# Self-attention's softmax maxima turned by 32x32 squares and two DRAM transfers instead of TensorE transposes, in a four-layer diffusion transformer

## The chip, the cores and the metric

The kernel runs on 1 core of one Trainium2 chip. The metric is the device time of one execution in microseconds, taken as the median of several; before the change it is 2573.73 us. All data is float32; some operands are float32r (a 4-byte format that TensorE multiplies faster), for which a value is split in a high and a low part so that nothing is lost.

## The reference

Sixteen batches of x [256 rows, 256 features] go through four layers. Layers 0, 2 and 3 are full: self-attention, cross-attention to a context of 120 rows, and an MLP. Layer 1 has cross-attention alone. Cut to a full layer and to layer 1:

```python
# layers 0, 2, 3 (16 heads of 16 features; N = 256 queries, S = 120 context rows)
mod = silu(cond) @ ada_w + ada_b                    # shifts, scales and gates, six rows
qkv = (ln(x) * (1 + scale_a) + shift_a) @ qkv_w + qkv_b
x = x + gate_a * (softmax(q @ k.T / 4) @ v @ proj_w + proj_b)
q = ln(x) @ q_w + q_b;  k, v = split(context @ kv_w + kv_b)
x = x + softmax(q @ k.T / 4) @ v @ cp_w + cp_b
x = x + gate_m * (gelu(mlp_in @ fc1_w + fc1_b) @ fc2_w + fc2_b)
# layer 1: adaptive layer norms of x and context, then the cross-attention line
```

The softmax subtracts each row's maximum. This kernel keeps that: it needs, for every query and head, the largest score over the keys.

## The kernel before, in words

**Jobs and steps.** The work on one batch in one layer is cut into steps, and each engine runs its part of the steps in one long order written out in tables of words (`START`, `TURN`, `WITH_L1`, `TAIL`). A word is a part and a step: P is the projection of self-attention's q, k and v, F its attention, A its output projection; R, G and B are the same for cross-attention; E is the MLP. A leading 1, as in 1G, means layer 1. One pass of a table is a turn; it works on different batches of all parts at once, so that TensorE has something to do while other engines finish a step. `TURN` is for turns without layer 1, `WITH_L1` for turns 3 to 21, in which layer 1's cross-attention (from turn 6 on) runs beside layer 0. There are 48 jobs of F and 64 of G, 16 of them of layer 1.

**Attention.** Steps S (L1287 on TensorE) multiply q with k, query rows on the partitions, into the four-bank PSUM tile `score`; VectorE reduces each to row maxima (`row_max`, L978). F has units S0 to S3, G has S0 and S1. `score` is one tile for all: the next unit on TensorE waits until the one before it is reduced. Steps T (L1309) multiply again, now with keys on the partitions, and L1314 subtracts the maxima inside PSUM, by a matmul of a selection matrix `sel` with `max_t`; ScalarE takes the exponential (`probs`, L1117). Steps PV (L1340) multiply with v, steps O (L1000 to L1011, VectorE) turn and normalise.

**The maxima.** Between S and T they must be turned: S leaves them with queries on the partitions, T needs them with heads on the partitions and queries along the row. Step X (VectorE, L987 and L990) negates them and splits them in a high and a low part, in `max_parts`, 8 columns of each group of 32. Step M transposes `max_parts` on TensorE (two 128x128 transposes by L1144, into one of three PSUM banks called the ring), and ScalarE copies the result to `max_t` (L1106). The first unit T0 waits for that copy.

**The ring.** The steps of most projections, norms and M take the three ring banks in turn; a step waits until the bank's last result was read.

**Queues.** All transfers are started by SyncE (SP) in order: the laying of q and k (L652, L661 to L663), loads of weights and context, and the gates `gate_now_P` and `gate_now_E` (L720, L721), 1 KB rows of DRAM spread to all partitions. `gate_now_P` waits for the product `gated` of A.PR (L1019 on VectorE), which reads its buffer. GpSimd (POOL) adds `gated` to x (L787, L793).

In the two tables the places that matter are

```python
TURN:     F.S3 E.H3 p.N P.gld A.PR F.X A.PR.d / G.S0 F.M B.PR B.PR.d R.C / G.S1 E.F20a E.F20b G.X / F.T0 ...
WITH_L1:  F.S2 P.gld E.H1 f.O1 E.H2 / F.S3 F.X 1R.LN E.RES E.H3 / 1G.S0 A.PR F.M A.PR.d /
          1G.S1 1G.X B.PR E.F20a / G.S0 E.F20b 1G.M B.PR.d / G.S1 E.F21a / 1G.T0 ... 1G.T1 ... F.T0
```

A word with `.d` is where SyncE, GpSimd and VectorE do their part of a step that TensorE and ScalarE did at the plain word. In the trace the places of M in `TURN` show TensorE in the order A.PR, G.S0, F.M, B.PR, R.C, G.S1.

Of the kernel before, what the change touches and what calls it, by code (L numbers as in the profile page):

```python
# [7 lines left out]
F32 = mybir.dt.float32  # L8
# [5 lines left out]
P = 128  # L14
# [4 lines left out]
NT = 256  # L19
# [14 lines left out]
CTX_LN = (False, True, False, True)  # L34

# [123 lines left out]

def turn(i, nb):  # L160
# [23 lines left out]
def sequence(nb):  # L184
# [11 lines left out]
    for r, m, step, n in steps:  # L196
        here = None
        if step in RING_STEPS:
# [61 lines left out]
def build_program(nc, a, out, nb=16):  # L260
# [9 lines left out]
    cross_order = {job: i for i, job in enumerate(cross_jobs)}  # L270
    normed_order = {job: i for i, job in enumerate(job for job in cross_jobs if CTX_LN[job[0]])}
# [8 lines left out]
    with ctx:  # L280
        def sb(name, shape, dt=F32):
# [7 lines left out]
        sel = sb("sel", [P, PAIRS])  # L289
        minus_half = sb("minus_half", [P, TT])  # L290
# [54 lines left out]
        max_parts = {r: sb(f"max_parts_{r}", [P, TT, P]) for r in "FG"}  # L345
        max_t = {r: sb(f"max_t_{r}", [P, NT]) for r in "FG"}
# [36 lines left out]
        m_psum = signals("m_psum", "FG")  # L383
# [11 lines left out]
        max_t_ready = signals("max_t_ready", "FG")  # L395
# [13 lines left out]
        max_parts_ready = signals("max_parts_ready", "FG")  # L409
        o_turned_ready = signals("o_turned_ready", "FG", 2)  # L410
# [18 lines left out]
        k_laid = semaphore("k_laid")  # L429
        x_stored = semaphore("x_stored")  # L430
# [154 lines left out]
        def _(sp):  # L585
# [211 lines left out]
        def _(dve):  # L797
# [6 lines left out]
                .then_inc(sel_ready, 1)  # L804

# [48 lines left out]
            for r, m, step, n, here in steps_d:  # L854
# [124 lines left out]
                elif step == "X":  # L979
                    src = row_max[r][:, :, :, :].rearrange("p t g c -> p (t g) c")  # L980
                    parts = max_parts[r][:, :, :].rearrange("p t (g w) -> p (t g) w", g=GROUPS)[:, :, 0:2 * PAIRS]\
# [3 lines left out]
                    m_psum[r].wait_before(dve, m, n)  # L985
# [6 lines left out]
                        .then_inc(max_parts_ready[r].sem, 1)  # L992
                elif step in ("O0", "O1"):
# [43 lines left out]
        def _(act):  # L1037
# [3 lines left out]
            for r, m, step, n, here in steps:  # L1041
# [61 lines left out]
                elif step == "M":  # L1103
# [36 lines left out]
        def _(pe):  # L1140
# [46 lines left out]
            for r, m, step, n, here in steps:  # L1187
# [103 lines left out]
                elif step == "M":  # L1291
# [4 lines left out]
                elif step[0] == "T" and step[1:].isdigit():  # L1296
# [4 lines left out]
                    if v == 0:  # L1301
                        pe.wait_ge(max_t_ready[r].sem, max_t_ready[r].after(m, n))
                        if m == 0 and n == 0:
                            pe.wait_ge(sel_ready, 1)
# [95 lines left out]
```

## Time and profile before

| what | value |
|---|---|
| median of 3 runs (lowest to highest) | 2573.73 us (2573.45 to 2574.57) |
| the profiled execution, its own time | 2577.71 us |
| its span in the trace | 2575.9 us |
| TensorE, busy | 2479.3 us, 96% |
| VectorE, ScalarE, GpSimd, busy | 72%, 49%, 18% |
| DMA queue of SyncE, share of 16 engines | 24.7% |

The busy shares say which engine could set the time. The view of waits says who waited for whom and how long in total. The timeline lists instructions in order of time with the idle time before them; a matmul's duration overlaps the next one's, so distances are read from start to start. The DMA view gives, for each transfer, the median time from its issue to its landing.

### The profile page before, as it was taken

The numbers are of one execution on the slowest core, as the hardware profiler recorded it, in microseconds if no ns is written. First come the engines' busy times: TensorE is split into PE (matmuls) and PEld (weight loads), VectorE is DVE, ScalarE is ACT, GpSimd is POOL, SyncE is SP. The second block draws the span as 40 slices with busy tenths as digits, with TensorE's granted clock in tenths as the row PEclk, the third lists the DMA queues.
The fourth block names the chain that finished last, engine by engine and source line by source line (L and its number), as shares of the span: only waits on it lengthen the run. The fifth ranks groups of instructions, "written<-read, shape, count | busy, mean of one in ns | idle before, by whom it ended". The sixth has DMA issues, their size and how long they took to land.

```text
span 2575.9 us, 66165 instructions
## 1 busy us (share of the span) xinstructions
PE 2479.3 (96%) x27466; PEld 1848.3 (72%) x27466; DVE 1858.5 (72%) x3532; ACT 1274.0 (49%) x1810; POOL 467.2 (18%) x510
## 2 busy tenths in 40 slices
PE   5779999999999999999999999999999999999998
PEld 3557777777777777777777777777777777777767
DVE  4767777777777777777777767777677677776752
ACT  1345544555555555555455554554555545445443
POOL 0111211212111211111121211211212212112121
PEclk7889999999999999999999999999999999999999
DMA  5322222222222223232122122132231222222211
GB/s 188 129 93 78 78 74 74 74 80 87 83 77 76 90 81 96 77 101 68 56 76 74 56 76 74 62 96 78 80 107 60 82 84 78 78 66 80 82 33 42
DMA packets 236749, 207.56 MB, mean 81 GB/s; under 512 B 87682, under 2 KB 222020, under 8 KB 236452
## 3 DMA queue, kind: packets, MB, share of 16 engines
q1 hardware_dynamic: 236452, 203.32, 24.7%
q8 instruction: 220, 3.60, 0.6%
q14 instruction: 77, 0.63, 0.1%
HBM read 58.34 MB, written 4.39 MB: 24 GB/s over the span
## 4 chain that ended last, share of the span: by engine, by line
PE 79%; DVE 12%; issue 3%; ACT 3%; SPq 2%; DMA 1%; POOL 1%; DVEq 0%; POOLq 0%; ACTq 0%
PE o_acc L1340 11%; PE score L1287 10%; PE ring L1371 10%; PE ring L1248 10%; PE ring L1362 10%; PE score L1309 8%; PE ring L1352 6%; DVE row_max_F L978 5%; DVE row_max_G L978 5%; PE ring L1144 4%; PE ring L1256 3%; PE score L1314 3%; PE ring L1268 2%; ACT probs L1117 2%; PE ring L1271 2%
## 5 line engine op out<-in xcount | busy, mean ns | idle before, releaser
L1117 ACT ACTIVATE probs<-score 120x2048 f32<-120x2048 f32 (+1 forms) x320 | 601.6, 1880 | 374.8 <-PE score L1314 368.0
L978 DVE TENSOR_REDUCE row_max_F<-score 128x8 f32<-128x2048 f32 x192 | 438.7, 2285 | 103.3 <-PE score L1287 102.8
L1371 PE MATMUL ring<-w_fc,h_t 128*128 128x256 f32 x1536 | 368.9, 386 | 1.0 <-ACT h_t L1128 1.0
L1362 PE MATMUL ring<-x_t_E,w_fc 128*128 128x256 f32 x1536 | 368.3, 386 | 0.0
L978 DVE TENSOR_REDUCE row_max_G<-score 128x16 f32<-128x1920 f32 x128 | 276.1, 2157 | 116.8 <-PE score L1287 116.8
L1128 ACT ACTIVATE h_t<-ring,cols 128x256 f32<-128x256 f32 x384 | 160.7, 470 | 341.1 <-PE ring L1362 341.0
L1362 PEld LDWEIGHTS ring<-x_t_E,w_fc 128*128 128x128 f32 x1536 | 280.8, 190 | 59.3 <-issue 20.3
L1000 DVE STREAM_TRANSPOSE o_turned<-o_acc 128x512 f32<-128x512 f32 x224 | 159.9, 714 | 220.3 <-PE o_acc L1340 220.3
L1371 PEld LDWEIGHTS ring<-w_fc,h_t 128*128 128x128 f32 x1536 | 282.5, 190 | 46.3 <-ACT h_t L1128 1.4
L1340 PE MATMUL o_acc<-probs,v_self 128*17 128x256 f32 x3072 | 204.3, 384 | 0.0
L793 POOL TENSOR_TENSOR x<-x,gated 128x256 f32<-128x256 f32 x96 | 70.3, 733 | 723.1 <-DVE gated L1032 723.1
L1248 PE MATMUL ring<-x_t_P,w_qk 128*128 128x256 f32 x768 | 197.8, 403 | 1.2 <-ACT x_t_P L1068 1.2
L1309 PE MATMUL score<-q_F,k_F 32*128 32x256 f32 x3072 | 166.6, 303 | 8.9 <-ACT probs L1117 5.7
L1309 PEld LDWEIGHTS score<-q_F,k_F 32*128 32x128 f32 x3072 | 119.3, 184 | 75.2 <-issue 55.7
L1248 PEld LDWEIGHTS ring<-x_t_P,w_qk 128*128 128x128 f32 x768 | 143.9, 197 | 35.2 <-issue 8.4
L1287 PEld LDWEIGHTS score<-k_F,q_F 32*128 32x128 f32 x3072 | 106.4, 188 | 84.2 <-DVE row_max_F L978 42.0
L1287 PE MATMUL score<-k_F,q_F 32*128 32x256 f32 x3072 | 146.3, 307 | 21.4 <-DVE row_max_F L978 18.5
L1287 PEld LDWEIGHTS score<-k_G,q_G 32*128 32x128 f32 x4096 | 125.3, 187 | 52.4 <-DVE row_max_G L978 28.0
L1287 PE MATMUL score<-k_G,q_G 32*128 32x120 f32 x4096 | 142.9, 277 | 14.8 <-DVE row_max_G L978 12.0
L787 POOL TENSOR_TENSOR x<-x,gated 128x512 f32<-128x512 f32 x48 | 60.8, 1267 | 423.0 <-DVE gated L1019 423.0
L1340 PE MATMUL o_acc<-probs,v_ctx 120*17 120x256 f32 x2048 | 135.5, 382 | 0.0
L1099 ACT ACTIVATE q_parts<-ring,cols 128x256 fp32r<-128x256 f32 x224 | 94.0, 472 | 80.9 <-PE ring L1248 78.9
(136 smaller groups left out, 3770.9 us busy)
## 6 DMA issues: line engine op xcount, KB each, us to landing
q_G<-q_parts SPq DMA_DIRECT2D x256, 128.0 KB, 2.1
q_F<-q_parts SPq DMA_DIRECT2D x192, 128.0 KB, 2.1
k_F<-k_parts SPq DMA_DIRECT2D x96, 256.0 KB, 2.5
k_F<-k_parts SPq DMA_DIRECT2D x192, 128.0 KB, 2.2
k_G<-k_parts SPq DMA_DIRECT2D x128, 120.0 KB, 2.2
k_G<-k_parts SPq DMA_DIRECT2D x256, 60.0 KB, 1.9
gate_now_P<-gate_rows SPq DMA_DIRECT2D x48, 256.0 KB, 3.2
gate_now_E<-gate_rows SPq DMA_DIRECT2D x48, 256.0 KB, 3.4
```

Of the source, the lines that this page charges most:

```text
L978: nc.vector.tensor_reduce(dst, src, AX.X, ALU.max).then_inc(row_max_ready[r].sem, 1)
L1000: nc.vector.transpose(o_turned[:, :, :, :].rearrange("p i b d -> p (i b d)"), o_acc[:, :])\
L1117: nc.scalar.activation(probs[v % 2][0:keys, :, :], score[0:keys, :].rearrange("p (h q) -> p h q", h=2 * GROUPS), ACT.Exp, scale=SCALE).the ...
L1128: last = nc.scalar.activation(h_t[:, c, :], ps[:, c % 2 * NT:(c % 2 + 1) * NT], ACT.Gelu_apprx_tanh, bias=col(m, "fc1", c))
L1144: return nc.tensor.transpose(dst, src, ident[0:rows_in, 0:rows_in])
L1248: last = mm(ps[:, c * NT:(c + 1) * NT], weight[:, k, at + c * P:at + (c + 1) * P], buffer(x_t, r, m, n)[:, k, :], start=k == 0, stop=k == ...
L1287: last = mm(score[:, col0:col0 + width], q_now[at, c, e, tile * P:(tile + 1) * P].bitcast(F32R), k_now[at, two, c, e, :].bitcast(F32R), st ...
L1309: mm(score[0:keys, g * BANK + e * NT:g * BANK + (e + 1) * NT], k_now[at, two, c, e, tile * P:tile * P + keys].bitcast(F32R), q_now[at, c, ...
L1340: last = mm(o_acc[32 * j:32 * j + HD + 1, i * NT:(i + 1) * NT], v_head, probs[v % 2][0:keys, 2 * j + i, :], start=tile == 0 and (i == 0 or ...
L1352: last = mm(ps[:, t * D:(t + 1) * D], buffer(o_t, r, m, n)[:, k, t * P:(t + 1) * P], weight[:, k, :], start=k == 0, stop=k == KC - 1)
L1362: last = mm(ps[:, c % 2 * NT:(c % 2 + 1) * NT], w_fc1[:, k, c * P:(c + 1) * P], buffer(x_t, r, m, n)[:, k, :], start=k == 0, stop=k == KC - 1)
L1371: last = mm(ps[:, 0:D], h_t[:, k, t * P:(t + 1) * P], w_fc2[:, k, :], start=k == 0, stop=k == MC - 1)
```

## The change

It concerns the maxima of self-attention from the fourth job on (45 of 48) and of layer 1's cross-attention (16 of 64). For these, X writes high and low parts packed in 32 columns, and VectorE transposes 128x64 in squares of 32x32. SyncE writes the squares to a DRAM tensor `max_rows` (32 heads' parts by 256 queries), at X, and at M reads it back into `max_t`, once for each of the four groups of partitions. TensorE's transposes and ScalarE's copy are gone there; the step M no longer takes a ring bank. T0 waits for the read. A second selection matrix, `sel_moved`, fits the new order of rows.

```diff
+def by_transfers(r, m, n, nb):
+    return (r == "F" and FULL_BEFORE[m] * nb + n >= 3) or (r == "G" and m == 1)
...
-        if step in RING_STEPS:
+        if step in RING_STEPS and not (step == "M" and by_transfers(r, m, n, nb)):
             here = at % RING
...
+        max_rows = {r: nc.dram_tensor(f"max_rows_{r}", [32, NT], F32, kind="Internal").ap() for r in "FG"}
...
+        max_turned = {r: sb(f"max_turned_{r}", [P, TT, 32]) for r in "FG"}
...
+                if step == "X" and by_transfers(r, m, n, nb):
+                    sp.wait_ge(max_turned_ready[r].sem, max_turned_ready[r].after(m, n))
+                    if moved_order[r][m, n] > 0:
+                        sp.wait_ge(max_laid[r].sem(m, n), max_laid[r].after(m, n) - 16)
+
+                    sp.dma_start(max_rows[r].rearrange("h (t a q) -> a h t q", t=TT, a=4), max_turned[r][:, :, :])\
+                        .then_inc(max_written[r].sem(m, n), 16)
+                elif step == "M" and by_transfers(r, m, n, nb):
+                    sp.wait_ge(max_written[r].sem(m, n), max_written[r].after(m, n))
+                    t_psum[r].wait_before(sp, m, n)
+                    sp.dma_start(max_t[r][:, :], max_rows[r].unsqueeze(0).to_broadcast([GROUPS, 32, NT]))\
+                        .then_inc(max_laid[r].sem(m, n), 16)
...
+            for g in range(GROUPS):
+                at = slice(32 * g, 32 * (g + 1))
+                last = nc.vector.tensor_reduce(pair_rows_moved[at, :], ident[at, 40 * g:40 * g + 2 * PAIRS]
+                                               .rearrange("p (c e) -> p c e", e=2), AX.X, ALU.add)
+            last.then_inc(pair_rows_ready, 1)
+            dve.wait_ge(pair_rows_ready, 2)
+            nc.vector.tensor_copy(sel_moved[:, :].bitcast(F32R), pair_rows_moved[:, :]).then_inc(sel_ready, 1)
...
+                    if by_transfers(r, m, n, nb):
+                        parts = max_parts[r][:, :, 0:32].rearrange("p t (b e) -> p t b e", e=2)
...
+                    if by_transfers(r, m, n, nb):
+                        dve.wait_ge(max_parts_ready[r].sem, max_parts_ready[r].after(m, n))
+                        if moved_order[r][m, n] > 0:
+                            dve.wait_ge(max_written[r].sem(m, n), max_written[r].after(m, n) - 16)
+                        nc.vector.transpose(max_turned[r][:, :, :],
+                                            max_parts[r][:, :, 0:32])\
+                            .then_inc(max_turned_ready[r].sem, 1)
...
-                elif step == "M":
+                elif step == "M" and not by_transfers(r, m, n, nb):
                     act.wait_ge(m_psum[r].sem, m_psum[r].after(m, n))
...
-                elif step == "M":
+                elif step == "M" and not by_transfers(r, m, n, nb):
                     pe.wait_ge(max_parts_ready[r].sem, max_parts_ready[r].after(m, n))
...
-                        pe.wait_ge(max_t_ready[r].sem, max_t_ready[r].after(m, n))
+                        if by_transfers(r, m, n, nb):
+                            pe.wait_ge(max_laid[r].sem(m, n), max_laid[r].after(m, n))
+                        else:
+                            pe.wait_ge(max_t_ready[r].sem, max_t_ready[r].after(m, n))
```

TensorE, the last turn with layer 1, from 1G.S0 to 1G.S1 (the brackets name the semaphores an instruction waits for), before:

```order
L1287 MATMUL score<-k_G,q_G 128x120 [waits k_laid,q_laid,row_max_ready_F]
L1287 MATMUL score<-k_G,q_G 128x120 x31
L1352 MATMUL ring<-w_proj,o_t_A 128x256 [waits o_t_ready_F,h_ready_E]
L1352 MATMUL ring<-w_proj,o_t_A 128x256 x3
L1144 MATMUL ring<-ident,max_parts_F 128x128 [waits max_parts_ready_F,h_ready_E]
L1144 MATMUL ring<-ident,max_parts_F 128x128
L1287 MATMUL score<-k_G,q_G 128x120 [waits row_max_ready_G]
```

and with the change:

```order
L1342 MATMUL score<-k_G,q_G 128x120 [waits k_laid,q_laid,row_max_ready_F]
L1342 MATMUL score<-k_G,q_G 128x120 x31
L1411 MATMUL ring<-w_proj,o_t_A 128x256 [waits o_t_ready_F,h_ready_E]
L1411 MATMUL ring<-w_proj,o_t_A 128x256 x3
L1342 MATMUL score<-k_G,q_G 128x120 [waits row_max_ready_G]
```

The two transposes are gone; what stands before and behind them waits for the same as before.

VectorE, a turn without layer 1, from the statistics of p.N to the reduction of G.S0, before and with the change:

```order
L825 TENSOR_SCALAR var_eps_P<-mean_var_P 128x2 [waits mean_ready_P]
L987 TENSOR_SCALAR max_parts_F<-row_max_F 128x8x4 [waits row_max_ready_F,m_psum_F]
L990 SCALAR_TENSOR_TENSOR max_parts_F<-row_max_F,max_parts_F 128x8x4 [waits max_hi_ready_F]
L1019 TENSOR_TENSOR gated<-ring,gate_now_P 128x512 [waits x_out_ready_E,gate_loaded_P0,pr_psum_A]
L978 TENSOR_REDUCE row_max_G<-score 128x16 [waits s_psum_G,max_parts_ready_G]
```

```order
L864 TENSOR_SCALAR var_eps_P<-mean_var_P 128x2 [waits mean_ready_P]
L1035 TENSOR_SCALAR max_parts_F<-row_max_F 128x2x16 [waits row_max_ready_F,max_turned_ready_F]
L1038 SCALAR_TENSOR_TENSOR max_parts_F<-row_max_F,max_parts_F 128x2x16 [waits max_hi_ready_F]
L1045 STREAM_TRANSPOSE max_turned_F<-max_parts_F 128x64 [waits max_written_F,max_parts_ready_F]
L1074 TENSOR_TENSOR gated<-ring,gate_now_P 128x512 [waits x_out_ready_E,gate_loaded_P0,pr_psum_A]
L1017 TENSOR_REDUCE row_max_G<-score 128x16 [waits s_psum_G,max_parts_ready_G]
```

The transpose stands ahead of the gated product, and with it of the reduction.

SyncE, the last turn with layer 1, with the change (before, `gate_now_P` is followed at once by `q_F`):

```order
L752 DMA gate_now_P<-gate_rows 128x512 [waits gate_stored,gated_ready_A,x_biased_P]
L696 DMA max_rows_F<-max_turned_F 4x64x32 [waits max_laid_F,max_turned_ready_F]
L701 DMA max_t_F<-max_rows_F 128x1x256 [waits t_psum_F,max_written_F]
L696 DMA max_rows_G<-max_turned_G 4x64x32 [waits max_laid_G,max_turned_ready_G]
L701 DMA max_t_G<-max_rows_G 128x1x256 [waits t_psum_G,max_written_G]
L671 DMA q_F<-q_parts 64x2x256 [waits t_psum_F,q_parts_ready_F]
```

Each read waits in the queue for its write; the first write comes behind the gate load. In turns without layer 1 the two rows of G are missing.

## Rows read from the trace of the kernel before

**Rows 1.** The page: busy times of the engines, and the chain that ended last.

```profile
PE 2479.3 (96%) x27466; PEld 1848.3 (72%) x27466; DVE 1858.5 (72%) x3532; ACT 1274.0 (49%) x1810; POOL 467.2 (18%) x510
...
PE 79%; DVE 12%; issue 3%; ACT 3%; SPq 2%; DMA 1%; POOL 1%; DVEq 0%; POOLq 0%; ACTq 0%
```

**Rows 2.** Stretches of one turn each; busy time (x instructions), granted clock, DMA.

```profile
317.13:377.60 60.47, 59.60 (x692) 44.20 (x691) 46.90 (x91) 31.42 (x45) 11.14 (x12) 1.00 0.25 78
...
1796.47:1843.03 46.56, 46.45 (x515) 34.94 (x511) 33.63 (x65) 23.90 (x34) 9.24 (x11) 1.00 0.22 71
```

**Rows 3.** Groups of instructions: step M's transposes on TensorE.

```profile
L1144 PE MATMUL ring<-ident,max_parts_G 128*128 128x128 f32 x128 | 25.6, 281 | 0.0
...
L1144 PE MATMUL ring<-ident,max_parts_F 128*128 128x128 f32 x96 | 20.3, 294 | 0.8 <-DVE max_parts_F L990 0.8
```

**Rows 4.** Timeline of TensorE, last turn with layer 1: start, duration, [idle before <-releaser].

```profile
1221.30 1.11 PE L1287 MATMUL score<-k_G,q_G 32*128 32x120 f32 x32 [0.47 <-DVE row_max_F L978]
...
1224.17 0.38 PE L1144 MATMUL ring<-ident,max_parts_F 128*128 128x128 f32 x2
1224.75 1.11 PE L1287 MATMUL score<-k_G,q_G 32*128 32x120 f32 x32 [0.19 <-DVE row_max_G L978]
...
1236.26 0.50 PE L1309 MATMUL score<-q_G,k_G 32*120 32x256 f32 x8 [0.34 <-DVE row_max_G L978]
```

**Rows 5.** Timeline of SyncE, the same turn.

```profile
1225.36 0.33 SPq L721 DMA_DIRECT2D gate_now_P<-gate_rows  x1
```

**Rows 6.** Timeline of TensorE, a turn without layer 1.

```profile
2028.38 1.11 PE L1287 MATMUL score<-k_G,q_G 32*128 32x120 f32 x32
...
2031.82 1.11 PE L1287 MATMUL score<-k_G,q_G 32*128 32x120 f32 x32
...
2036.51 0.51 PE L1309 MATMUL score<-q_F,k_F 32*128 32x256 f32 x8
```

**Rows 7.** Timeline of VectorE and SyncE (SPq), the same turn.

```profile
2028.41 0.19 DVE L990 SCALAR_TENSOR_TENSOR max_parts_F<-row_max_F,max_parts_F 128x32 fp32r<-128x32 f32 x1
2028.53 0.69 DVE L1019 TENSOR_TENSOR gated<-ring,gate_now_P 128x512 f32<-128x512 f32 x1
...
2029.28 0.33 SPq L721 DMA_DIRECT2D gate_now_P<-gate_rows  x1
...
2029.61 2.16 DVE L978 TENSOR_REDUCE row_max_G<-score 128x16 f32<-128x1920 f32 x1 [0.39 <-PE score L1287]
```

**Rows 8.** Waits, 317 to 1283 us and 1328 to 2448 us: total, times, longest.

```profile
PE score L1287 <- DVE row_max_G L978: 6.1, 32, 0.2
...
PEld score L1287 <- DVE row_max_G L978: 6.1, 24, 0.3
```

**Rows 9.** Timeline of TensorE, an early turn and the tail.

```profile
214.20 0.38 PE L1144 MATMUL ring<-ident,max_parts_F 128*128 128x128 f32 x2
...
2449.06 0.41 PE L1144 MATMUL ring<-ident,max_parts_F 128*128 128x128 f32 x2 [0.82 <-DVE max_parts_F L990]
```

**Rows 10.** Groups of instructions: VectorE's transposes.

```profile
L1000 DVE STREAM_TRANSPOSE o_turned<-o_acc 128x512 f32<-128x512 f32 x224 | 159.9, 714 | 220.3 <-PE o_acc L1340 220.3
...
L1011 DVE STREAM_TRANSPOSE o_t_B<-o_norm 128x256 f32<-128x256 f32 x128 | 57.0, 445 | 4.4
```

**Rows 11.** Waits, whole execution.

```profile
DVE gated L809 <- ACT gated L1039: 4.7, 1, 4.7
```

**Rows 12.** DMA issues: count, KB each, median us to landing.

```profile
k_G<-k_parts SPq DMA_DIRECT2D x128, 120.0 KB, 2.2
...
gate_now_P<-gate_rows SPq DMA_DIRECT2D x48, 256.0 KB, 3.2
...
context<-in_ctx_dram SPq DMA_DIRECT2D x32, 120.0 KB, 2.3
...
gate_rows<-h_t SPq DMA_DIRECT2D x6, 32.0 KB, 2.1
...
v_bias<-in_L_xcond_b_qkv_dram SPq DMA_DIRECT2D x1, 128.0 KB, 4.3
```

More of the change, by code:

```diff
@@ L270, in build_program @@
     cross_order = {job: i for i, job in enumerate(cross_jobs)}
+    max_moved = {r: [job for job in jobs if by_transfers(r, *job, nb)]
+                 for r, jobs in (("F", list(self_order)), ("G", cross_jobs))}
+    max_made = {r: [job for job in jobs if not by_transfers(r, *job, nb)]
+                for r, jobs in (("F", list(self_order)), ("G", cross_jobs))}
     normed_order = {job: i for i, job in enumerate(job for job in cross_jobs if CTX_LN[job[0]])}
@@ L382, in build_program @@
         s_psum = signals("s_psum", "FG", {"F": 4, "G": 2})
-        m_psum = signals("m_psum", "FG")
+        m_psum = {r: Signal(semaphore(f"m_psum_{r}"), 1, {job: i for i, job in enumerate(max_made[r])}) for r in "FG"}
         t_psum = signals("t_psum", "FG", {"F": 4, "G": 2})
@@ L394, in build_program @@
         k_high_ready = signals("k_high_ready", "FG")
-        max_t_ready = signals("max_t_ready", "FG")
+        max_t_ready = {r: Signal(semaphore(f"max_t_ready_{r}"), 1, m_psum[r].order) for r in "FG"}
         probs_ready = signals("probs_ready", "FG", {"F": 4, "G": 2})
@@ L409, in build_program @@
         max_parts_ready = signals("max_parts_ready", "FG")
+        moved_order = {r: {job: i for i, job in enumerate(max_moved[r])} for r in "FG"}
+        max_turned_ready = {r: Signal(semaphore(f"max_turned_ready_{r}"), 1, moved_order[r]) for r in "FG"}
         o_turned_ready = signals("o_turned_ready", "FG", 2)
@@ L429, in build_program @@
         k_laid = semaphore("k_laid")
+        max_written = {r: Turns([semaphore(f"max_written_{r}")], moved_order[r]) for r in "FG"}
+        max_laid = {r: Turns([semaphore(f"max_laid_{r}")], moved_order[r]) for r in "FG"}
         x_stored = semaphore("x_stored")
@@ L980, in _ @@
                     src = row_max[r][:, :, :, :].rearrange("p t g c -> p (t g) c")
+                    if by_transfers(r, m, n, nb):
+                        src = row_max[r][:, :, :, :].rearrange("p t g c -> p t (g c)")
                     parts = max_parts[r][:, :, :].rearrange("p t (g w) -> p (t g) w", g=GROUPS)[:, :, 0:2 * PAIRS]\
                         .rearrange("p b (c e) -> p b c e", e=2)
+                    if by_transfers(r, m, n, nb):
+                        parts = max_parts[r][:, :, 0:32].rearrange("p t (b e) -> p t b e", e=2)
                     if m == 0 and n == 0:
                         dve.wait_ge(const_ready, CONSTS)
-                    m_psum[r].wait_before(dve, m, n)
+                    at = (self_order if r == "F" else cross_order)[m, n]
+                    if at > 0:
+                        em, en = (list(self_order) if r == "F" else cross_jobs)[at - 1]
+                        turned = max_turned_ready[r] if by_transfers(r, em, en, nb) else m_psum[r]
+                        dve.wait_ge(turned.sem, turned.after(em, en))
                     dve.wait_ge(row_max_ready[r].sem, row_max_ready[r].after(m, n))
```

8 lines of the change are left out of this document (6 added, 2 removed).

## The prediction

> **What bounds the kernel now.** Read first the busy shares and the chain of waits: TensorE is busy for 2479.3 of 2575.9 us, and 79% of the chain that ended last lies on it [rows 1]. So only what shortens TensorE's own sequence, or a wait in it, can shorten the kernel. The table of stretches then shows two kinds of turn, at full clock: with layer 1's attention beside layer 0's (60.47 us, TensorE busy 59.60), and without (46.56, busy 46.45) [rows 2]. There are 16 turns of the first kind and 25 of the second, each alike to hundredths; three shorter turns stand before them. What matters is thus where TensorE still waits inside a turn.
>
> The timeline answers that (unit names as in the section on the kernel). In a turn with layer 1, the units 1G.S0 and 1G.S1 start at 1221.30 and 1224.75 [rows 4]. Between them TensorE has a projection (A.PR) and the maxima's transposes (F.M), and then still waits 0.19 us for VectorE's maximum. The interval of 3.45 is VectorE's: 1.11 of matmuls, 0.12 to hand over, 2.16 of reduction, 0.05 to hand back; the same parts can be read in the other kind of turn, 2028.38 to 2031.82 [rows 6, 7]. The transposes of layer 1's maxima (1G.M) stand in the same way inside the next such interval, before G.S1. The view of waits counts 32 waits of 0.19 over the 16 turns, which is both places of each, and 24 waits of a quarter us over 24 whole turns without layer 1 [rows 8]. **Nearly all transposes that the change removes stand where TensorE goes on to wait for VectorE anyway.**
>
> **What the change removes.** 61 steps M: 45 of self-attention, 16 of layer 1. TensorE's busy time for them is 20.3/48 = 0.42 us a step for F and 25.6/64 = 0.40 for G [rows 3], or 45 x 0.42 + 16 x 0.40 = 25.3 us. Of these steps 32 + 25 = 57 lie in the covered intervals: the wait behind them grows by what they took, and S1 starts when it did. Worth 0. If VectorE's reduction were not there to cover it, it would all be won; that is a rival below. Four steps have no such cover. In the three turns before layer 1 starts the transposes (one at 214.20, 0.38) are followed by a projection without a wait [rows 9]; the next step starts before they end, so I take 0.3 each, bounds 0 and 0.4: 0.9 us. In the tail, F15.M waits 0.82 for max_parts and then takes about 0.3 before G13.S0 [rows 9]: 1.1 us, bounds 0 and 1.2. Sum: -2.0 us.
>
> Also gone are 61 ScalarE copies of the turned maxima. ScalarE is at 49% and idle around those copies in the covered places; its exponentials start when TensorE releases them. Worth 0. The steps M no longer take a place in the ring of three PSUM banks, so each later ring step finds a bank that was given up no later than before: no new wait, and no ring wait of size in the list. Worth 0.
>
> **What it adds on VectorE.** One transpose of 128x64 in each moved X, with a wait on the instruction ahead. No such size is in the trace. The transposes of 128x512 (714 ns) and 128x256 (445) [rows 10] give 1.05 ns an element; carried down to 64 elements that is 0.24 us, and about 0.05 for the wait. Bounds 0.19 (the small operation ahead of it, [rows 7]) and 0.45 (the smaller transpose shown). In turns without layer 1 it stands between max_parts (2028.41) and the gated product (2028.53, 0.69 long), behind which the reduction of G.S0 is queued. That reduction sat idle 0.39 us before TensorE released it [rows 7], so a delay of 0.29 is covered; at the upper bound 0.11 is left over, 25 x 0.11 = 2.8 us. I take 0. With layer 1 X stands in gaps of VectorE. The four small reductions and the cast at the start fall into VectorE's wait of 4.7 us for the conditioning vector [rows 11]. Worth 0; 1.5 us, some five small operations of 0.2 to 0.5, if they did not.
>
> **What it adds on SyncE and the DMA queue.** 61 writes of 32 KB to DRAM in pieces of 128 bytes, and 61 reads of 128 KB. The queue of SyncE runs in order: gate_now_P, write, wait for the write, read. The gate load waits for the gated product and so starts at 2029.28 [rows 7], after X. In the changed kernel this is 0.28 later: 2029.56, 0.33 to issue, so the write is issued at 2029.95. TensorE reaches F.T0 at 2036.51 [rows 6]. With 0.1 for two hand-overs, **write plus read, each from issue to landing, may take 6.45 us**. Past that, T0 starts late in each of 25 turns.
>
> Write: the nearest row is gate_rows<-h_t, 32 KB to DRAM, 2.1 us; many small pieces (k_G, 256 of 480 bytes) took 2.2; behind a gate load that is still moving I add 0.5. I take 2.7, bounds 2.1 and 3.4 (the gate load's 3.2 with a hand-over more) [rows 12]. Read: bounds 2.3 (context, 120 KB from DRAM) and 4.3 (one row spread to all partitions, amid weight loads); nearest is gate_now_P, rows of DRAM spread to 128 partitions, 3.2 for twice the bytes [rows 12]. I take 3.0. Sum 5.7, so 0.75 us to spare: no wait. At the bounds, 7.7 is 1.25 late, 25 x 1.25 = 31 us.
>
> The Trainium skill (DMA: Bandwidth & Descriptors, Anatomy of one DMA) gives about 2.0 us fixed for a transfer plus its bytes at 436 GB/s, for another issuing engine; an estimate by it would be 2.1 + 2.3 = 4.4 for the pair, with 2 us to spare, and the same forecast.
>
> In turns with layer 1 four transfers stand in a chain: gate load at 1225.36 [rows 5], F's write at 1225.74, landed 1228.4, F's read issued until 1228.9; layer 1's maxima are turned at about 1228.95 (1224.75 + 1.11 + 0.12 + 2.16 + X), written by 1231.7, laid by 1234.8. 1G.T0 stands at 1236.26, held there by VectorE [rows 4]: 1.5 us to spare. F.T0 comes after both 1G.T units. At the upper bounds (3.4, 3.4, 4.3) it is laid at 1237.2, 1.0 late, 16 us over 16 turns. While SyncE waits for the writes, its next work is the laying of q, ten us later: nothing is held up.
>
> **Sum.** Profiled execution: 2577.71 - 2.0 = 2575.7. It lies 4.0 above the median of the runs, 2573.73, so I forecast a median of **2571.7 us**. A measurement of this kernel tells about 0.2% (5.1 us) from no change; the forecast is within that.
>
> **Rivals.**
> (a) The wait for the turned transposes gives way to one for the laid maxima at F.T0. For it: the gate load ahead in the queue, pieces of 128 bytes that no row shows as a write, and only 0.75 us to spare. If the write takes its upper bound of 3.4 and the read 3.5, a little over the gate load's 3.2, the pair takes 6.9, 0.45 late, 25 x 0.45 = 11 us: 2583. It decides from a pair of 6.45 on; from 6.7 on the kernel is measurably slower; the upper bounds give 2571.7 + 31 + 16 = 2619. Against it: the queue is only a quarter busy, and each of the two transfers would have to be well over its nearest row. Chance 0.20. The Trainium skill (same page, Specifications) says that pieces under 512 bytes are handled by read-modify-write; by that rule the write would be the slow one, as in (a). No row here shows a write in such pieces to DRAM.
> (b) VectorE's longer queue puts the reduction behind G.S0 late, at 0.45 for the transpose: 2571.7 + 2.8 = 2574.5, still no change. Chance 0.06.
> (c) The removed TensorE time is all won, because the intervals are not really VectorE's: 25.3 + 0.8 us, 2547.6. For it: TensorE is at 96%. Against it: the 56 counted waits right behind these steps. Chance 0.08; a partial gain past 5 us has 0.02 more.
> (d) The forecast: 0.64.
>
> **How the numbers follow.** Faster 0.10 is (c) and its part. Slower 0.20 is (a). Same 0.70 is (b) and (d). The likeliest case alone runs from 2570 to 2575. The range takes in most of (a), up to a pair of 7.0 us (25 x 0.55 = 14): 2569 to 2586.
>
> **What would show it.** Right: turns keep their 60.4 and 46.6 us; the wait of L1287 for row_max_G grows by about 0.4 in turns with layer 1 and 0.3 in the others; ScalarE loses 61 copies; the transpose takes about 0.24; TensorE waits for no landing of max_t before T0; the tail is a microsecond shorter. Wrong: a wait before the first score matmul of T0 on max_t<-max_rows means (a), a reduction of G.S0 that is released by VectorE itself (b), an S0 to S1 interval under 3.4 (c). Turns of another length without any of these would break the whole reading.

## The result, and the profile after

The changed kernel takes 2612.44 us in the median of four runs (2609.09 to 2616.92), the kernel before 2573.59 beside it: a ratio of 1.0146, 95% interval 1.0134 to 1.0158. It is slower by 1.5%, outside the range, and on the side of rival (a), whose own price was 2583. The profiled execution has a span of 2615.0 us, 39.1 more than before.

The page's busy shares and its chain answer to [rows 1]:

```profile
PE 2475.3 (95%) x27344; PEld 1842.3 (70%) x27344; DVE 1871.4 (72%) x3598; ACT 1250.9 (48%) x1749; POOL 467.2 (18%) x510
...
PE 68%; DVE 12%; DMA 12%; issue 4%; ACT 2%; SPq 2%; POOL 0%; DVEq 0%; POOLq 0%; ACTq 0%
```

TensorE has 122 instructions fewer and hardly less busy time. What moved is the chain: 11 points of it went from TensorE to the DMA. The table of stretches answers to [rows 2]: one turn with layer 1 and one without, each from one `gate_now_P` issue to the next (duration; busy time and instructions of TensorE, its weight loads, VectorE, ScalarE, GpSimd; granted clock, where 1.00 is full; DMA share and GB/s):

```profile
317.56:379.31 61.75, 59.17 (x695) 43.74 (x694) 46.93 (x92) 30.66 (x43) 11.14 (x12) 1.00 0.27 82
...
2066.45:2113.80 47.35, 46.34 (x509) 34.82 (x509) 33.74 (x66) 23.53 (x33) 9.24 (x10) 1.00 0.25 79
```

Measured from one `gate_now_P` issue to the next, the 16 turns with layer 1 took 993.97 us against 963.58, the 24 whole ones behind them 1131.5 against 1120.0: 30.4 and 11.5 more. The stretch before them is 0.8 shorter, what comes after them 2.1 shorter. That is the 39.1. The view of waits of TensorE, 317 to 1310 us and then 1310 to 2490 us (total, times, longest), says what the turns wait for:

```profile
PE score L1368 <- DMA max_t_G<-max_rows_G: 29.6, 16, 4.3
PE score L1342 <- DVE row_max_G L1017: 13.1, 32, 0.4
...
PE score L1368 <- DMA max_t_F<-max_rows_F: 8.5, 15, 0.8
PE score L1342 <- DVE row_max_G L1017: 5.0, 25, 0.2
```

Here are two readings. The waits for `row_max_G` answer to [rows 8]: with layer 1 there are still 32 places, and their wait has grown from 6.1 us to 13.1. The time of the removed transposes became a wait, as forecast. New are the waits of the units T0 for the laid maxima: all 16 of 1G, and 15 of F. The timeline of a turn without layer 1 (start, duration, [idle before <-releaser]; SPq are issues on SyncE) shows the transfers on their way:

```profile
2065.30 1.11 PE L1342 MATMUL score<-k_G,q_G 32*128 32x120 f32 x32
...
2066.45 0.34 SPq L752 DMA_DIRECT2D gate_now_P<-gate_rows  x1
...
2066.88 0.58 SPq L696 DMA_DIRECT2D max_rows_F<-max_turned_F  x1
...
2068.74 1.11 PE L1342 MATMUL score<-k_G,q_G 32*128 32x120 f32 x32 [0.20 <-DVE row_max_G L1017]
...
2069.78 0.57 SPq L701 DMA_DIRECT2D max_t_F<-max_rows_F  x1
...
2074.24 0.51 PE L1368 MATMUL score<-q_F,k_F 32*128 32x256 f32 x8 [0.73 <-DMA max_t_F<-max_rows_F]
```

The interval from S0 to S1 is 3.44 us, as before. The write took 2.9 from its issue to that of the read, the read about 4.4 from there (4.46 to T0, with a hand-over). The same in the last turn with layer 1:

```profile
1251.14 1.11 PE L1342 MATMUL score<-k_G,q_G 32*128 32x120 f32 x32 [0.41 <-DVE row_max_G L1017]
1251.75 0.35 SPq L752 DMA_DIRECT2D gate_now_P<-gate_rows  x1
...
1252.20 0.57 SPq L696 DMA_DIRECT2D max_rows_F<-max_turned_F  x1
...
1255.02 0.25 DVE L1045 STREAM_TRANSPOSE max_turned_G<-max_parts_G 128x64 f32<-128x64 f32 x1
1255.26 0.57 SPq L701 DMA_DIRECT2D max_t_F<-max_rows_F  x1
...
1255.91 0.52 SPq L696 DMA_DIRECT2D max_rows_G<-max_turned_G  x1
...
1260.07 0.53 SPq L701 DMA_DIRECT2D max_t_G<-max_rows_G  x1
...
1264.20 0.50 PE L1368 MATMUL score<-q_G,k_G 32*120 32x256 f32 x8 [1.89 <-DMA max_t_G<-max_rows_G]
```

Layer 1's write is issued behind F's read and takes 4.2 us, its own read 4.1 more. The reduction ahead of T0 was done at about 1262.6, so T0 is 1.5 late. Last, the DMA in the 5 us from 2069 to 2074, around the read of the turn without layer 1 (40 slices of 0.125 us; share of the 16 engines in tenths, GB/s):

```profile
DMA  2100000000000000000004300122222222220200
GB/s 62 30 4 0 0 0 0 0 0 0 0 0 0 0 0 0 0 0 0 0 0 16 16 0 8 57 98 98 90 98 98 98 98 98 98 74 0 66 0 0
```

The read of 128 KB runs at 98 GB/s, on about a quarter of the engines, though next to nothing else is moving.

### The profile page after: what moved, and what is told of

Read it like the earlier page. It is cut to its first block, busy times and chain, and to the rows that moved or that the text cites. A ratio compares the mean times of both kernels' runs of the same rounds, so it can differ in the third digit from the quotient of the medians.

```text
span 2615.0 us, 66105 instructions
## 1 busy us (share of the span) xinstructions
PE 2475.3 (95%) x27344; PEld 1842.3 (70%) x27344; DVE 1871.4 (72%) x3598; ACT 1250.9 (48%) x1749; POOL 467.2 (18%) x510
## 4 chain that ended last, share of the span: by engine, by line
PE 68%; DVE 12%; DMA 12%; issue 4%; ACT 2%; SPq 2%; POOL 0%; DVEq 0%; POOLq 0%; ACTq 0%
PE o_acc L1399 11%; PE ring L1303 11%; PE ring L1421 8%; PE score L1368 8%; PE score L1342 7%; PE ring L1430 7%; DVE row_max_F L1017 6%; DMA max_rows_F<-max_turned_F 3%; PE ring L1199 3%; PE ring L1311 3%; PE score L1373 3%; DMA max_rows_G<-max_turned_G 3%; PE ring L1411 3%; PE ring L1323 2%; DMA max_t_G<-max_rows_G 2%
## 5 line engine op out<-in xcount | busy, mean ns | idle before, releaser
L1303 PE MATMUL ring<-x_t_P,w_qk 128*128 128x256 f32 x768 | 202.7, 411 | 1.2 <-ACT x_t_P L1123 1.2
L1303 PEld LDWEIGHTS ring<-x_t_P,w_qk 128*128 128x128 f32 x768 | 146.9, 201 | 36.1 <-issue 8.6
L888 DVE SCALAR_TENSOR_TENSOR q_parts<-ring,cols,q_parts 128x256 fp32r<-128x256 f32 x224 | 97.5, 476 | 70.4 <-ACT q_parts L1154 70.4
L1368 PE MATMUL score<-q_G,k_G 32*120 32x256 f32 x2048 | 111.2, 303 | 37.6 <-DMA max_t_G<-max_rows_G 29.6
```

Source lines behind the costliest of these rows:

```text
L888: last = nc.vector.scalar_tensor_tensor(out=parts[:, 1, c, 0:width].bitcast(F32R), in0=src[:, c * width:(c + 1) * width], scalar=row_col(m ...
L1303: last = mm(ps[:, c * NT:(c + 1) * NT], weight[:, k, at + c * P:at + (c + 1) * P], buffer(x_t, r, m, n)[:, k, :], start=k == 0, stop=k == ...
L1368: mm(score[0:keys, g * BANK + e * NT:g * BANK + (e + 1) * NT], k_now[at, two, c, e, tile * P:tile * P + keys].bitcast(F32R), q_now[at, c, ...
```

## The experiments

The expectations name the theories by letters; what each letter stands for is said where it is first used. "Before", or the number in brackets, is the kernel before on the same chip in the same job. Spans are those of one profiled execution each. The kernel before has 2575.9, but within one job its spans lie up to 9 us apart, and in e4, whose transfers begin only with layer 1, the stretch ahead of the turns is 3.1 us shorter. So differences of a few us are read from medians or from single turns, not from spans.

### Is the loss all in the waits of T0?

Theory A: TensorE waits at T0 for late transfers, and nothing else is lost. Theory B: the transfers and VectorE's longer order cost turn time by themselves. First, the wait moved from T0 to the last unit T. The units ahead of it have no maxima then and subtract a row of q, so this kernel is good for its time alone:

```diff
-                            pe.wait_ge(max_laid[r].sem(m, n), max_laid[r].after(m, n))
...
+                    last_unit = v == (3 if r == "F" else 1)
+                    if last_unit and by_transfers(r, m, n, nb):
+                        pe.wait_ge(max_laid[r].sem(m, n), max_laid[r].after(m, n))
```

> TensorE waits for the laid maxima before the last T unit of a job (T3 of F, T1 of G) instead of before T0; the earlier units subtract a row of q in place of the maxima, and the exponential has a scale of 1e-6 of its own so that all stays finite (the result is not the reference's). All transfers stay as in the changed kernel. Theory A (the whole loss is T0 standing for the landing): about 2571, the changed kernel's 2612 less the waits, that is the 2571.7 forecast, give or take 3. Theory B (the loss also comes from what the transfers do to others: queue, score, VectorE): it stays above 2585.

Measured: 2576.61 us (2575.28), ratio 1.0000, interval 0.9991 to 1.0010; span 2573.8. All transfers run as in the changed kernel, and the whole loss is gone, within 0.1%. Theory B falls. Theory A's own figure, 2571 give or take 3, was missed by 2.6 us: the kernel before was 1.7 higher here than in the first job, and the 2 us of gain that the figure holds did not show.

Second, `gate_now_P` issued behind both transfers. In the tables the word `P.gld` moves:

```diff
-F.S3 E.H3 p.N P.gld A.PR F.X A.PR.d
-G.S0 F.M B.PR B.PR.d R.C
+F.S3 E.H3 p.N A.PR F.X A.PR.d
+G.S0 F.M P.gld B.PR B.PR.d R.C
...
-F.S2 P.gld E.H1 f.O1 E.H2
+F.S2 E.H1 f.O1 E.H2
...
-G.S0 E.F20b 1G.M B.PR.d
+G.S0 E.F20b 1G.M P.gld B.PR.d
```

> Only the order in SyncE's queue changes: the load of gate_now_P goes behind the write and the read (in turns with layer 1 behind both pairs). Theory A: without layer 1 the write starts 1.2 us earlier, which is more than the 0.5 lost per turn, so those 11.5 us come back; with layer 1 F's pair is done before layer 1's write starts, whose own 2.9 + 4.3 ends at about 1236.2 on the clock of the old turn, within 0.1 of when T0 is due: 2570 to 2576. Theory B: the order of the queue matters little, since the read is slow by itself: 2600 or more.

Measured: 2574.95 (2575.28), ratio 0.9996 (0.9987 to 1.0005); span 2574.9. The timeline of a turn without layer 1:

```profile
2074.04 1.11 PE L1342 MATMUL score<-k_G,q_G 32*128 32x120 f32 x32
...
2074.58 0.57 SPq L696 DMA_DIRECT2D max_rows_F<-max_turned_F  x1
2076.93 0.56 SPq L701 DMA_DIRECT2D max_t_F<-max_rows_F  x1
2077.60 0.42 SPq L752 DMA_DIRECT2D gate_now_P<-gate_rows  x1
...
2082.17 0.51 PE L1368 MATMUL score<-q_F,k_F 32*128 32x256 f32 x8
```

The write now takes 2.35 us from its issue to the read's, half a microsecond less. It is issued 0.54 us after the start of G.S0 in place of 1.58, since it no longer stands behind the gate load, which waits for the gated product. The read is no faster, but T0 doesn't wait. So some 1.6 us in the queue decides here: T0 was 0.8 late, and now has about 0.8 to spare. In the whole execution one wait for laid maxima is left, 0.84 us in the tail; and with the others gone, the change gains nothing measurable.

### The two halves alone

```diff
-    return (r == "F" and FULL_BEFORE[m] * nb + n >= 3) or (r == "G" and m == 1)
+    return r == "F" and FULL_BEFORE[m] * nb + n >= 3
```

> Self-attention's 45 jobs go by transfers, layer 1's 16 by TensorE as before. Theory A: turns with layer 1 are as long as before (F.T0 comes late there), turns without keep their 0.5 us each: 2573.6 - 2.8 + 11.5 = 2582. Theory B (the transposes' absence or the transfers cost in every turn): near 2600.

Measured: 2583.78 (2575.28), ratio 1.0033 (1.0022 to 1.0043); span 2582.5. The turns with layer 1 are back at 60.5; the sixteen waits left are F's, in the others. The other half:

```diff
-    return (r == "F" and FULL_BEFORE[m] * nb + n >= 3) or (r == "G" and m == 1)
+    return r == "G" and m == 1
```

> Only layer 1's 16 jobs go by transfers. Theory A (layer 1's pair is late because it queues behind F's slow read, 4.1 instead of 2.9 for the write): alone it is laid before T0, 2573.6, at most 5 more. Theory B (layer 1's pair is too slow by itself): most of the 30 us of the turns with layer 1 stay, 2590 or more.

Measured: 2575.96 (2575.28), ratio 1.0002 (0.9993 to 1.0012); span 2574.7. Alone, layer 1's transfers make one late turn, and its write takes 2.4 us in place of 4.1 (medians of 16). The halves cost 8 and 0, together 39: layer 1's loss needs F's read ahead of its write in the queue.

### Why is the read slow?

Theories for 98 GB/s: O, the outer dimension of 4 (four groups of partitions) makes it slow; F (the letter here, not the attention), DRAM that was written just before is slow to read; S, the same rows read several times are slow. In four kernels self-attention's read takes old rows of the input x in place of `max_rows`. In these the maxima of F are not used: TensorE subtracts a row of q and the exponential is scaled by 1e-6, so they too are good for their times alone. Each of these kernels ran once; the kernel before beside r1 to r4 has a span of 2576.7. Layer 1's read stays as changed. The sources, r1 to r4:

```diff
+                                 a["x"][n][0:P, :])
...
+                                 a["x"][n].rearrange("(g h) d -> g h d", g=GROUPS)[:, 0:32, :])
...
+                                 a["x"][n][0:32, :].unsqueeze(0).to_broadcast([GROUPS, 32, NT]))
...
+                                 a["x"][n][0:1, :].to_broadcast([P, NT]))
```

> F's read of 128 KB takes 128 different rows of the input x, one block, in place of the 32 fresh rows four times (maxima unused, exponential's scale 1e-6 of its own, so the result is not the reference's; T0 waits for the landing as before). The read took 4.3 us in the changed kernel. Three causes stand against each other: F, the rows were only just written; S, four readers share each row; O, the transfer's outer dimension is 4, and it uses few engines. All three say here: about 2.3 us, like the context's load, no wait at T0 of F in turns without layer 1, and turns of 46.6 us again.

> The same, but four blocks of 32 rows with gaps between them: different rows, old data, outer dimension 4. O: still about 4.3 us, DMA at some 98 GB/s, T0 waits as in the changed kernel. F and S: about 2.3 us.

> The same, but 32 old rows of x spread four times, the very form of the changed kernel's read. F: about 2.3 to 3 us. S and O: about 4.3.

> The same, but one old row of x spread to 128 partitions. S: 4 us or more, longer than with four readers. F and O: about 2.3 to 3.2.

| | read | span | read issued in | waits of T0 for F's read |
|---|---|---|---|---|
| r1 | 128 rows in one piece | 2577.4 | 0.33 us | none |
| r2 | four blocks of 32 rows, gaps between | 2611.7 | 0.60 | 11.3 us, 25 times |
| r3 | 32 old rows, four times | 2606.2 | 0.60 | 7.2 us, 18 times |
| r4 | one row, 128 times | 2580.9 | 0.33 | none |

r2 reads 128 different old rows and is as slow as the change: O stands. r3 is the changed kernel's read but for the age of its rows, and still makes T0 wait: F, as the whole cause, falls. It is no slower than r2, so four readers for each row cost nothing that these runs show. With 128 readers it is otherwise: r4 has no late T0, but it too moves only 90 GB/s, and lands after 3.0 us in place of r1's 2.0.

Whether it is the outer dimension's size, or merely that there is a third one, three more kernels tell, again with one run each: the gapped read in 16, 8 and 2 blocks (r7, r6, r8), for instance

```diff
-                                 a["x"][n].rearrange("(g h) d -> g h d", g=GROUPS)[:, 0:32, :])
+                                 a["x"][n].rearrange("(g h) d -> g h d", g=16)[:, 0:8, :])
```

> As r2_static_gapped (self-attention's read takes 128 rows of the input x with a gap behind each block; the maxima are not used, TensorE subtracts rows of q instead and the exponential is scaled by 1e-6), but in sixteen blocks of 8 rows in place of four of 32. Same bytes, same number of dimensions, more gaps. Theory N (a transfer is spread over as many DMA engines as its outer dimension allows; with an outer dimension of 4 the rows show a share of 0.2 of the engines and 98 GB/s, the plain read 0.8 to 0.9 and up to 350): here the read goes over all engines, 200 GB/s or more, lands after 2.0 to 2.5 us, and the span is that of the plain read, 2577 to 2581. Rival (the third dimension or the gaps make it slow, whatever the outer size): 98 GB/s again, issue 0.60, span 2606 to 2614.

> As r7_static_sixteen with eight blocks of 16 rows. Theory N: eight engines, DMA share 0.4 to 0.5 and 196 GB/s during the read, landing between those of 4 and 16 blocks, span 2577 to 2600. Rival: as with four blocks, 2606 to 2614.

> As r7_static_sixteen with two blocks of 64 rows. Theory N: two engines, share 0.1 and 49 GB/s, 128 KB take 2.7 us in place of 1.3, so the read lands at least 1.3 us later than with four blocks and TensorE waits in every turn: 45 times 1.3 or more on top of 2611, span 2650 to 2720. Rival: as with four blocks, 2606 to 2614.

Measured spans: 2576.7 with 16 blocks, 2585.6 with 8, 2611.7 with 4, 2720.4 with 2 (the kernel before beside these: 2572.8, beside that with 4 blocks 2576.7). The DMA in 4 us from 0.5 us after one read's issue (slices of 0.1 us), for 2 blocks:

```profile
DMA  0000000001000000112001111133001111111111
GB/s 0 0 0 0 0 0 0 0 10 51 10 0 0 10 20 31 51 51 41 20 31 41 41 61 41 41 41 102 20 31 41 51 41 51 51 41 51 51 41 51
```

for 4 (r2):

```profile
DMA  0000000001000121012222222222100000000000
GB/s 0 0 0 0 0 0 0 0 10 41 10 20 31 41 41 51 31 51 72 102 102 82 102 102 92 102 92 92 41 0 0 0 0 0 0 0 0 0 0 0
```

for 8:

```profile
DMA  0000000009801003555442000000000000001000
GB/s 0 0 0 0 0 0 0 0 0 61 72 10 10 0 31 123 205 195 205 174 154 72 0 0 0 0 0 0 0 0 0 0 0 0 0 0 82 0 0 0
```

and for 16:

```profile
DMA  0000000002756973000000000000000003000000
GB/s 0 0 0 0 0 0 0 0 0 72 174 154 215 328 267 103 0 0 0 0 0 0 0 0 0 0 0 0 0 0 0 0 0 82 0 0 0 0 0 0
```

(The 9 and the 8 at the start of the view of 8 blocks are a few packets that took up to 0.6 us each.) The usual slices hold 41 to 51, 92 to 102 and 154 to 205 GB/s, at a tenth, a fifth and a half of the engines; with 16 blocks the read is over in 0.7 us, and its highest slice has 328 at nine tenths. That is theory N of the expectations: the size of the outer dimension sets how many of the 16 engines carry the transfer. The packets of these reads agree. Each read is 128 packets of 1 KB, most of them 46 ns long, and closes with 2, 4, 8 or 16 packets of 4 bytes; in the changed kernel 4 of these close the read, and 4 the write. The third dimension by itself costs a little as well: 16 blocks take 0.61 us to issue and land after 2.6, the plain read 0.33 and 2.0. The Trainium skill (DMA: Bandwidth & Descriptors, Why a DMA increments its semaphore by 16 and not by 1) states this rule: the number of engines is the largest up to 16 that divides the slowest dimension of both sides. The rows agree at 2, 4, 8 and 16. The Trainium skill's figure for the fixed part (same page, Anatomy of one DMA) gave the prediction's estimate of 4.4 us for write and read; measured are 7.3.

The same seven kernels show what the read does to the transfer behind it. Layer 1's write, issued directly behind F's read, takes 5.9 us behind 2 blocks, 4.2 behind 4, 3.1 behind 8, 2.5 behind 16, 2.4 behind the plain read and 2.7 behind the row spread to 128 (medians of 16 turns).

### The read in four transfers

If the cause is the outer dimension, four reads of [32, 256], one for each group, should help:

```diff
-                    sp.dma_start(max_t[r][:, :], max_rows[r].unsqueeze(0).to_broadcast([GROUPS, 32, NT]))\
-                        .then_inc(max_laid[r].sem(m, n), 16)
+                    for g in range(GROUPS):
+                        sp.dma_start(max_t[r][32 * g:32 * (g + 1), :], max_rows[r]).then_inc(max_laid[r].sem(m, n), 16)
```

> The changed kernel with the read as four transfers of [32, 256], one for each group of partitions, in place of one with outer dimension 4. Theory O (the outer dimension of 4 makes the read slow): each lands about 2.0 us after its issue as the plain read of 128 rows did, the last issue is some 1.2 us after the first, so 3.2 in all against 4.3, the waits at T0 go in both kinds of turn: 2571 to 2578. Rival (each small transfer takes 0.6 to issue and 2 or more, so little is won, and with layer 1 SyncE is held up longer): 2590 or more.

Measured: 2584.27 (2574.65), ratio 1.0041 (1.0026 to 1.0057); span 2582.4. Between the two expectations: of the changed kernel's span, 32.6 of the 39.1 us came back. The waits that are left, over the whole execution, and the queue in a turn with layer 1:

```profile
PE score L1368 <- DMA max_t_G<-max_rows_G: 10.0, 8, 1.9
...
PE score L1368 <- DMA max_t_F<-max_rows_F: 0.6, 3, 0.2
```

```profile
440.70 0.57 SPq L696 DMA_DIRECT2D max_rows_G<-max_turned_G  x1
443.06 1.70 SPq L702 DMA_DIRECT2D max_t_G<-max_rows_G  x4
```

Layer 1's write is down from 4.2 us to 2.4 now that F's read is quick. But four issues take 1.70 us in place of 0.53, and in eight of the sixteen turns with layer 1, at first every second one, the maxima still come 0.2 to 1.5 us too late. Why in these was not found.

### What the removed transposes are worth

Theory D: they can be won only where nothing else covers them. The four uncovered self-attention places alone:

```diff
+    return r == "F" and FULL_BEFORE[m] * nb + n in (3, 4, 5, 47)
```

> Transfers only for the four jobs whose TensorE transposes have no wait behind them (F of turns 3, 4, 5 and the tail). By the prediction's step on uncovered places: 1 us at the start and 1 to 1.8 in the tail, so 2571 where the kernel before has 2573.7, ratio 0.9990 (0.9985 to 0.9995). A rival (the tail's T0 then waits for its read, 4.3 us): no gain.

Measured: 2574.91 (2574.65), ratio 1.0000 (0.9991 to 1.0008); the interval leaves room for the 2 us, and does not show them. Turn by turn, the three at the start are 0.9 us shorter than before, as counted, and again in e9; e4, which has no such transfers there, has none of it. The tail's 1 us isn't shown: over the runs with a transfer there the tail is from 2.1 us shorter to 1.4 longer. Then beside them layer 0's cross-attention, whose transposes stand in no reduction's shadow, with its X put earlier in the table:

```diff
-1G.T1 R.N e.A P.Q.d 1G.PV0 R.RES G.X 1G.O0 P.K
+1G.T1 G.X R.N e.A P.Q.d 1G.PV0 R.RES 1G.O0 P.K
...
+    return (r == "F" and FULL_BEFORE[m] * nb + n in (3, 4, 5, 47)) or (r == "G" and m != 1 and 1 <= FULL_BEFORE[m] * nb + n <= 19)
```

> Transfers where something waits for ScalarE's copy: the ordinary cross-attention (G) of turns 3 to 21, whose T0 stands 0.99 for max_t_G behind an exponential, and the four uncovered jobs of F. X of G is moved ahead of R.N, so that its write is issued before q's laying. Without the copy T0 is due when F.T1's exponential has ended, 0.4 earlier: 19 x 0.4 = 7.6, and 2.5 of the four jobs: 2563.5. Rival (write, four layings of q and the read of 4.3 us do not fit between X and T0, 10 us): no gain or slower, 2574 or more.

> The same with the read as four transfers. If both the layer-0 place and theory O hold: 2563.5 as above, with more to spare. If the read was late in the kernel above and O holds, this one is the faster. Rival: k's laying is held up by the four issues: slower than the one above.

Measured: 2578.14 (2574.65), ratio 1.0016 (1.0007 to 1.0025), and with four reads 2575.69, ratio 1.0004 (0.9995 to 1.0013). Both missed 2563.5; the four reads are the faster of the two, as the expectation had it for a read that comes late. The timeline of e7 has three waits for the maxima in all, in the three turns before layer 1 starts:

```profile
186.60 0.79 PE L1368 MATMUL score<-q_G,k_G 32*120 32x256 f32 x8 [4.38 <-DMA max_t_G<-max_rows_G]
...
239.34 0.79 PE L1368 MATMUL score<-q_G,k_G 32*120 32x256 f32 x8 [4.20 <-DMA max_t_G<-max_rows_G]
...
293.52 0.50 PE L1368 MATMUL score<-q_G,k_G 32*120 32x256 f32 x8 [2.50 <-DMA max_t_G<-max_rows_G]
```

Those turns are 9.7 us longer than before, while fifteen turns with layer 1 take 60.2 in place of 60.5. So the three go back to TensorE's transposes:

```diff
-    return ... (r == "G" and m != 1 and 1 <= FULL_BEFORE[m] * nb + n <= 19)
+    return ... (r == "G" and m != 1 and 4 <= FULL_BEFORE[m] * nb + n <= 19)
```

> The routing is that of e7_cross_of_layer0 (all in the order of the tables with X of layer 0's cross-attention earlier), but the three cross-attention jobs before layer 1 starts (full jobs 1 to 3) go back to TensorE's transposes; the sixteen beside layer 1 and the four uncovered self-attention places keep the transfers. In the trace of e7 TensorE waited three times for the laid maxima of G, 4.4, 4.2 and 2.5 us, all in those three turns, which were 9.7 us longer than before (51.4, 54.0, 55.3 against 47.9, 49.8, 53.3), while its fifteen turns with layer 1 took 60.2 against 60.5. If TensorE's transposes can be won at places that nothing else covers, and the transfers cost nothing where their cover is long (the theory), those turns fall back, the sixteen keep their 0.25 us each and the four places their 2.2: span 2568 to 2570, median 5 to 7 us below the kernel before of the same job. If what e7 lost lies elsewhere (the rival), the span stays at 2575 to 2578 and the waits that are gone come back in another place.

Measured: 2571.01 (2575.47), ratio 0.9982 (0.9973 to 0.9991); span 2568.9. That is 4.5 us by the medians, a little under the 5 to 7 that were expected. A turn of it in the table of stretches:

```profile
440.00:500.20 60.20, 59.33 (x690) 44.07 (x689) 46.91 (x92) 31.15 (x44) 11.17 (x12) 1.00 0.27 82
```

The sixteen turns with layer 1 are 0.28 us shorter each, 4.5 in all. The kernel before has no run with G.X in its new place in the table alone, but the trace tells the two edits apart: in the turn shown, measured from `gate_now_P`, TensorE's steps agree with those of before within 0.01 us up to where the transposes of G.M stood, and from there on they come 0.28 earlier. This routing beats both kernels: twenty places in place of 61, chosen by what covers them. The slow read of an outer dimension of 4 is in it too; it does no harm where T0 comes late enough.

## Why the prediction was wrong

**Right: what the removal is worth.** 57 of the 61 steps were set at 0, since VectorE's reduction bounds the interval from S0 to S1. The interval stayed at 3.44 us, and the waits behind it grew from 6.1 to 13.1 us in the turns with layer 1. With the late transfers out of the way (e1, e2) the kernel stands at before's time within 0.1%, and rival (c) with its 25 us falls. The four uncovered places were put at 2.0 us. The 0.9 of the first three is there, 0.7 in the changed kernel and 0.9 in e5; the 1.1 of the tail is not shown by any run.

**Right: VectorE and ScalarE.** The transpose was taken at 0.24 us, and it takes 0.245. No reduction of G.S0 came late, so rival (b) falls.

**Wrong: the step "I take 3.0. Sum 5.7, so 0.75 us to spare: no wait".** The pair had 6.45 us. The write was taken at 2.7 and took 2.9, the read was taken at 3.0 and took 4.4: 7.3 in all. In the sum's own terms, the price of the read was too small by 1.4, and that of the write by 0.2. The nearest row chosen for the read was `gate_now_P`, rows spread to 128 partitions. It resembled the read in what it moves, not in its shape: it has no outer dimension of 4. The bound of 4.3, set by an unlike transfer, was the right number, by luck. With the measured pair the text's own sum gives 7.3 - 6.45 = 0.85 late and 25 x 0.85 = 21 us. The turn shown has that 0.8 (47.35 us against 46.56), but it is among the latest: waits were counted in 15 turns, 8.5 us in all.

**Wrong: layer 1's chain, "1.5 us to spare".** It was written with each transfer at its price alone: 2.7 for the write. In the last such turn the write was issued 0.08 behind the end of the issue of F's read, which is 0.6 later than the text had it, and took 4.2, 1.5 more than its price; the read took 1.1 more. The three together, less the 1.5 to spare, are a little over the 1.5 by which T0 was late. The write was slow because F's read was still moving on few engines: behind a read of as many bytes in 2, 4, 8 and 16 blocks it takes 5.9, 4.2, 3.1 and 2.5, and e4, where that read is absent, has 2.4 and one late turn of sixteen. Even the upper bounds (3.4, 3.4, 4.3; 1.0 late) missed this, since they took a queue for a list of independent prices. T0 was late by 29.6 us less the 5.5 that VectorE held it before (16 times 0.34): 24.1 in sum, against 16 at the bounds.

**Missing: what a late T0 does to the clock.** Of the 30.4 us of these turns 6.3 are left. The table of stretches for the 4 us from T0 on (columns as above) has twelve of sixteen at full clock and four not:

```profile
885.48:889.48 4.00, 4.00 (x32) 2.85 (x32) 1.62 (x7) 1.88 (x1) 1.48 (x2) 0.69 0.01 4
...
1073.43:1077.43 4.00, 4.00 (x32) 3.00 (x32) 1.72 (x7) 1.88 (x1) 1.50 (x2) 0.66 0.01 2
1139.33:1143.33 4.00, 4.00 (x31) 3.30 (x32) 0.00 (x0) 1.88 (x1) 0.00 (x0) 0.57 0.00 0
...
1264.20:1268.20 4.00, 4.00 (x36) 2.85 (x36) 1.60 (x7) 1.88 (x2) 1.44 (x2) 0.71 0.01 4
```

The column before the last two is the granted clock: 0.57 to 0.71, so that part of each stretch ran at the lower of the two levels, 1.2 GHz in place of 2.4. TensorE had stood idle for 1.8 to 4.3 us before. Eight matmuls of L1303 took 3.06 to 3.44 us there and 1.99 elsewhere. By the clock these stretches lost 4 x (0.31 + 0.34 + 0.43 + 0.29) = 5.5 us. In three of them the low clock lasts beyond the 4 us: over 8 us each of the four has 0.79, which is 4 x 8 x 0.21 = 6.7, the rest. The clock fell once more in the first turn without layer 1: a wait of 1.60 us for `probs` (0.35 before) and eight matmuls that took 3.26 us behind it, 2.5 in all. This wait is no late T0, for e1 has it too (1.72). ScalarE stood behind the laying of `k_F` there, and why that came later is open. With the 8.5 us of waits these are 11.0 of the other turns' 11.5.

**The chances.** Rival (a) named the mechanism, the point from which it decides (6.45) and, at its upper bounds, 2619, near the 2612 that came. That nearness is luck: it had 16 us for the turns with layer 1 and 31 for the others, and 30.4 and 11.5 came. It had 0.20 because "each of the two transfers would have to be well over its nearest row"; one of them was enough. The pair had two unseen shapes and 0.75 us of slack, a ninth of its length. The rule of the Trainium skill that the section on the slow read names (Why a DMA increments its semaphore by 16 and not by 1) would have said that write and read run on four engines; it was not brought in. The other rule of the Trainium skill, weighed in rival (a) (Specifications: pieces under 512 bytes are handled by read-modify-write), did not decide: the write in such pieces took 2.35 us with nothing ahead of it, near its nearest row of 2.1, and the slow one was the read, in pieces of 1 KB.

## What to carry to other kernels

When work moves from a busy engine to transfers, ask first what the engine waits for behind the removed instructions: here 57 of 61 removals were worth nothing, while sixteen of the twenty places without cover gained 0.28 us each. Price a transfer by a row of its own shape, its outermost dimension above all, and price a chain of transfers on one queue as a chain, each behind the one that is still moving. Where the slack is a ninth of an unseen sum, the case in which it does not suffice deserves more than one chance in five, and its price includes what an idle TensorE loses in clock afterwards.

## What the runs showed of the hardware

- The same 128 KB from DRAM (r8, r2, r6, r7): some 50 GB/s with an outer dimension of 2, 100 with 4, up to 205 with 8 and 328 with 16, closed by 2, 4, 8 and 16 packets of 4 bytes; landing after 2.0 us as 128 plain rows (r1), 2.6 as 16 blocks. One row spread to 128 partitions (r4): 90 GB/s, 3.0 us.
- A write of 32 KB in pieces of 128 bytes, from its issue to that of the read that waits for it: 2.35 us alone (e2), 2.9 behind a gate load of 256 KB, 5.9, 4.2, 3.1 and 2.5 behind a read of 128 KB with an outer dimension of 2, 4, 8 and 16.
- The longest single wait of T0, 4.3 us, came in the one turn with layer 1 in which a load of 1 MB (`w_fc`) was issued between F's write and its read; layer 1's write took 7.0 us there, and 4.0 in e4, whose one late turn this is.
- In the changed kernel, of sixteen waits of 1.0 to 4.3 us before layer 1's T0, four were followed by a lower granted clock. A wait of 2.65 us was not, one of 1.77 was; what tells them apart is open.
